# Another order for the row scatters behind the last attention: seven leftovers ahead of the last shift, one batch whole ahead of the next

## The reference

```python
x = x + _L1_attn_ref(_layernorm(x), ...)              # causal attention, 16 heads, 4 groups
x = x + _L1_ffn_ref(_layernorm(x), ...)

def _L1_ffn_ref(hidden, ...):
    logits = flat @ router_w.T                            # 2048 x 32
    scores = jnp.sqrt(jax.nn.softplus(logits))
    _, idx = jax.lax.top_k(scores + expert_bias, K)       # 4 experts for each token
    topv = jnp.take_along_axis(scores, idx, axis=1)
    topv = topv / (topv.sum(axis=-1, keepdims=True) + 1e-20)
    ...
    for each expert: out += p[:, None] * (silu(clip(x @ wg.T)) * clip(x @ wu.T)) @ wd.T
    return out + shared expert
```

## Time and profile before

| | us |
|---|---|
| median of 3 runs | 605.25 |
| lowest and highest run | 604.24, 608.36 |
| span of the profiled execution, first to last instruction | 624.5 |
| TensorE busy in it | 550.5 (88%) |
| VectorE busy | 433.0 (69%) |
| ScalarE busy | 346.5 (55%) |
| GpSimd busy | 241.2 (39%) |

### The profile page before, as it was taken

How to read it: one execution, slowest core, us unless ns; L and a number is a source line. 1 busy time by engine, 2 the same in 40 slices (tenths; PEclk the granted TensorE clock), 3 DMA queues, 4 the chain that set the end, 5 groups by cost and what they waited for, 6 DMA issues and landing times.

```text
span 624.5 us, 14114 instructions
## 1 busy us (share of the span) xinstructions
PE 550.5 (88%) x4231; PEld 390.9 (63%) x4232; DVE 433.0 (69%) x1298; ACT 346.5 (55%) x898; POOL 241.2 (39%) x341
## 2 busy tenths in 40 slices
PE   9998799999879989989998888866589999989996
PEld 4665455665458754666666665534367787778775
DVE  5678858888147886677788683535667777778755
ACT  3533657776826578456675456513146565656672
POOL 2533000000153213266544435556735555555530
PEclk9999979999999999999999899778799999999998
DMA  8599707000680005766505162235545454445498
GB/s 252 179 304 331 211 1 207 3 3 3 192 219 1 2 1 166 209 206 183 229 19 206 62 229 71 70 137 219 170 126 140 140 159 144 151 135 154 143 396 328
DMA packets 49554, 95.24 MB, mean 153 GB/s; under 512 B 8596, under 2 KB 40540, under 8 KB 46940
## 3 DMA queue, kind: packets, MB, share of 16 engines
q1 hardware_dynamic: 41820, 75.34, 39.4%
q0 software_dynamic: 7680, 19.21, 8.2%
HBM read 58.54 MB, written 35.59 MB: 151 GB/s over the span
## 4 chain that ended last, share of the span: by engine, by line
PE 54%; DVE 20%; issue 9%; ACT 6%; DMA 4%; POOL 3%; another core or an unknown queue 2%; SPq 1%; DVEq 0%; ACTq 0%; POOLq 0%
PE banks L1731 7%; PE banks L1513 6%; PE banks L1469 5%; PE banks L1322 4%; PE banks L1742 4%; PE banks L1534 4%; DVE mx L2087 3%; DVE mx L2090 3%; PE banks L1399 3%; PE banks L1794 2%; PE banks L1328 2%; DMA arena<-negT 2%; PE banks L1720 2%; DMA pvs<-rows_by_expert 2%
## 5 line engine op out<-in xcount | busy, mean ns | idle before, releaser
L1162 ACT ACTIVATE arena<-banks 128x512 f32<-128x512 f32 (+1 forms) x256 | 130.1, 550 | 83.3 <-PE banks L1513 45.8
L982 POOL DMA_INDIRECT results_by_rank<-attn_w,goes x80 | 77.3, 966 | 72.2 <-issue 47.9
L1513 PE MATMUL banks<-arena 98*128 98x256 bf16 (+1 forms) x512 | 88.6, 267 | 15.9 <-DVE arena L2186 3.8
L2087 DVE TENSOR_REDUCE mx<-banks 128x4 f32<-128x1024 f32 x64 | 76.0, 1220 | 18.1 <-PE banks L1469 18.0
L922 POOL DMA_INDIRECT rows_by_expert<-arena,bpb x64 | 63.2, 987 | 57.6 <-ACT arena L1162 22.4
L1469 PE MATMUL banks<-arena 96*128 96x256 bf16 (+1 forms) x512 | 81.5, 263 | 4.2 <-DVE mx L2087 2.5
L1731 PE MATMUL banks<-arena,attn_w 128*128 x320 | 84.4, 387 | 0.3 <-issue 0.3
L1513 PEld LDWEIGHTS banks<-arena 98*128 98x128 bf16 x512 | 43.2, 100 | 49.7 <-ACT arena L1162 15.0
L2090 DVE TENSOR_REDUCE mx<-banks 128x4 f32<-128x1024 f32 (+1 forms) x48 | 57.7, 1221 | 22.3 <-PE banks L1473 20.2
L1469 PEld LDWEIGHTS banks<-arena 96*128 96x128 bf16 x512 | 49.9, 99 | 20.0 <-issue 6.0
L1731 PEld LDWEIGHTS banks<-arena,attn_w 128*128 128x128 f32 x320 | 55.6, 194 | 5.1 <-issue 0.7
(11 more groups left out here) (253 smaller groups left out, 1095.7 us busy)
## 6 DMA issues: line engine op xcount, KB each, us to landing
arena<-parts_dram SPq DMA_DIRECT2D x72, 256.0 KB, 4.1
pvs<-rows_by_expert SPq DMA_DIRECT2D x80, 130.0 KB
parts_dram<-arena SPq DMA_DIRECT2D x24, 384.0 KB, 4.8
arena<-results_by_rank SPq DMA_DIRECT2D x6, 1024.0 KB, 10.3
arena<-in SPq DMA_DIRECT2D x2, 2304.0 KB
rows_by_expert<-zero SPq DMA_DIRECT2D x1, 4160.0 KB, 23.6
arena<-in SPq DMA_DIRECT2D x2, 1920.0 KB
arena<-in SPq DMA_DIRECT2D x3, 768.0 KB
```

Source lines behind the costliest of these rows:

```text
L982: pool.indirect_dma_start(ys, bass.IndirectOffsetOnAxis(ap=goes[:, j % 4:j % 4 + 1], axis=0), yb[j % 4], None).then_inc(y_stored[j % 4], 16)
L1162: act.activation(p_ring[n][:, i % P_RING, :], st_bank[RING_AT[n]["s", b, s] % 3][:, 0:P_WIDTH[n]], ACT.Exp, scale=HD ** -0.5).then_inc(exp ...
L1513: ins = pe.matmul(dst[:, at:at + SEQ - q0], keys, q_rows(n, slice(0, ROWS), s, b, q0, SEQ - q0), start=True, stop=(n == 0 or b < POOL_MASKS))
L2087: ins = dve.tensor_reduce(out, src.rearrange("p (q h k) -> p q h k", q=QT, k=nk), AX.X, ALU.max)
```

## The change

The leftovers are split once instead of twice: seven come ahead of the last shift, four behind it, and the wait for the divisions is gone (`scale_rows` still waits for its own statistics). Batch 4 is scattered whole, picks 3, 2, 1, 0, before batch 5, which follows whole in the same order. The number of scatters, their rows and what they raise stay the same. The whole diff:

```diff
--- before.py
+++ after.py
@@ -171,6 +171,7 @@
 RANKS_AT = {(4, 3): 0, (6, 2): 1, (7, 7): 2}
 UP_AT, CLIP_AT, LOGISTIC_AT, HIDDEN_AT, DOWN_AT, ADD_AT = ((6, 7), (6, 9)), (6, 10), ((7, 1), (7, 2), (7, 3)), (7, 5), ((7, 9), (7, 11)), (7, 12)
 SCATTERS = ((68, 13, 8, 16), (99, 11, 8, 16), (122, 9, 8, 5))
+BEHIND_LAST = 7
 
 
 LOGISTICS = 2
@@ -955,19 +956,13 @@
                     for j, n in scatters_at(b * HEADS + h):
                         scatter_nth(j, n, b * HEADS + h)
             tiles = [(BATCHES[2][0] * QT + n // TOPK, n % TOPK) for n in range(SCATTERS[2][3], 4 * TOPK)]
-            for t, k in tiles[:2]:
-                scatter(t, k)
-            pool.wait_ge(divided[1], SEQS * QT)
-            for t, k in tiles[2:4]:
+            for t, k in tiles[:BEHIND_LAST]:
                 scatter(t, k)
             scale_rows(7)
-            for t, k in tiles[4:]:
+            for t, k in tiles[BEHIND_LAST:]:
                 scatter(t, k)
-            scatter_picks(3, (3, 2))
-            scatter_picks(4, (3, 2))
-            for k in (1, 0):
-                scatter_picks(3, (k,))
-                scatter_picks(4, (k,))
+            scatter_picks(3, (3, 2, 1, 0))
+            scatter_picks(4, (3, 2, 1, 0))
             pool.wait_ge(placed[0], 2 * TILES * 16)
             pool.wait_ge(picks_placed, 2)
             pool.nop().then_inc(picks_placed, 1)
```

## The result

The changed kernel takes 613.28 us (median of four runs, 609.34 to 615.94) against 604.75 us (603.81 to 608.36) of the kernel before beside it: a ratio of 1.0126, interval 1.0087 to 1.0166. That is slower by over 1%, and above the upper end of the predicted range, 608.2. Run again at the end of the study, beside 23 runs of the kernel before, it gave 1.0117 [1.0067, 1.0167].

What follows compares the result with a forecast made beforehand. TensorE waits for GpSimd's scatters between attention and the loop: 3.1 us gained at block 4, less a delay of 3.5 - 0.7 - 0.8 = 2.0, gives 1.1 off 605.25, written 604.0 us; range 600.3 to 608.2.

Steps and rivals of the forecast that it cites:

- The gap decides: Between attention and the block loop, 411 to 455 us, TensorE is busy 30.44 of 44 us and waits for GpSimd.
- The second hole: GpSimd idle 3.15 us before 437.98, waiting for the fifth batch's slots; the fourth batch's scatters were to fill it.
- the two unnamed waits: Waits without a named releaser: ScalarE's 5.77 us before its last exponential, VectorE's 3.61 us for the last ranks.
- The term of 5.0 us for an earlier last level: GpSimd's level saying all picks are placed was to come at 449.7 instead of 454.7 us, 5.0 us earlier.
- The levels raised by ScalarE stay where they are within 0.3 us.: ScalarE's two lower levels, at 443.4 and 444.3 us, were to move by no more than 0.3 us.
- Block 4 waits for the last level: In the loop, block 4 starts 9.89 us after block 0, held by GpSimd's last level at 454.7 us.
- the 3.1 us that were to reach the loop: Block 4 could start at 454.1 instead of 457.24 us, so only 3.1 of the 5.0 us help TensorE.
- hold 3.5 us: Five scatters beside the last values and transposes make TensorE's results 3.5 us late, bounds 0 and 4.5.
- second way: If TensorE isn't held, the last shift waits for the five scatters until 417.6 instead of 415.0: delay 2.6 us.
- The rival on the losing side: 17%: TensorE held 4.5 us in its last values and transposes, perhaps 3.6 more at the last ranks; 606.7 to 610.3 us.
- The whole gain arrives: 17%: TensorE isn't held in its last attention step, the stall at the last ranks vanishes; gain 5.7, 599.5 us.
- It doesn't do what it says: 8%: SyncE's slow register operations, not the last level, release block 4; moved scatters only shift the slow stretch: 605.25 us.

Runs made afterwards that it cites:

- e1: The kernel before, unchanged, profiled a second time: ratio 0.9989, span 604.8 us.
- e3: Kernel before with only the fourth batch whole ahead of the fifth, leftover scatters and wait for the divisions kept: ratio 1.0065, 610.86 us.
- e2: Kernel before with seven leftover scatters ahead of the last shift, no wait for the divisions, old order of batches: ratio 1.0072, 610.46 us.
- e5: Kernel before with three leftover scatters ahead of the last shift, no wait for the divisions, old order of batches: ratio 1.0036, 606.25 us.
- e8: Kernel before without the wait for the divisions, all picks 3 and 2 first, three ahead of the last shift, others filling gaps: ratio 1.0034, 605.89 us.
- e10: Kernel before with the wait for the divisions kept, the shift directly behind it, nine leftover scatters following: ratio 1.0035, 606.46 us.
- e4: Changed kernel with three instead of seven leftover scatters ahead of the last shift, new order of batches: ratio 1.0057, 609.55 us.

## Why the prediction was wrong

**The gap decides, and TensorE waits there for what GpSimd does.** Right: the loss lies in that stretch; the loop behind its first matmul lasts as long as before within 1 us (614.2 - 442.29 = 171.9 after, 604.8 - 433.75 = 171.05 in e1).

**The second hole and the two unnamed waits were taken for the kernel's.** This is the step that failed first. The prediction noted that the profiled execution was 19.2 us longer than the median and went on to make the sum in it. In e1 neither the 3.15-us hole nor the unnamed waits of 5.77 and 3.61 us exist; GpSimd is the busy one all through, so a scatter that goes ahead of another delays it by 1.3 us, and there was no idle time to fill. The term of 5.0 us for an earlier last level had nothing to come from. It shrinks to this: counted from the fifth batch's slots, the last level comes 441.7 - 422.5 = 19.2 us behind them in e1 and 445.7 - 429.9 = 15.8 after, 3.4 us sooner, but it isn't what the loop waits for.

**"The levels raised by ScalarE stay where they are within 0.3 us."** Wrong, and the costliest step of the second half. The fourth batch's high picks were put ahead of the fifth's low ones, and the prediction counted on the hole to take them. With no hole, the second level went from 430.3 - 422.5 = 7.8 us behind the slots to 11.3 (after) and 13.8 (e3), past its 2.4 us of slack. Even in the profile of before that slack was to be read: ScalarE's levels at 443.4 and 444.3 stood 447.35 - 444.3 = 3.05 us ahead of block 0, and the prediction never asked what comes when they are later.

**Block 4 waits for the last level.** Wrong: in e1 block 4 starts at 439.54, 2.2 us ahead of the level, and block 6's transfer, the only one that TensorE waits for there (0.40 us), starts at 440.12 in the chain, ahead of 441.7 too. The first load that follows the level is block 7's, and for it TensorE doesn't wait. That 455.14 follows 454.7 in the first profile was read as a release from the times alone. The floor of 4 x 1.68 = 6.7 us for four blocks was too low as well, since they take 7.88 us in e1 with no wait for the level; the granted clock there is 0.50 from 430.8 to 437.4. After, the level is sooner by 3.4 us of the slots' count, and still block 4 follows block 0 by 448.60 - 440.02 = 8.58 us, against 439.54 - 431.66 = 7.88 in e1 (9.89 in the earlier trace rows). So the 3.1 us that were to reach the loop were not to be had, and with them went the predicted gain of 1.1 us.

**What the five scatters cost.** The term "hold 3.5 us" (bounds 0 to 4.5) fell: 6.26 us from the last exponential to the statistics after, against 6.74 in e1. The "second way" to the same term had the right mechanism, the shift waiting behind the five scatters until the last of them, but sized it at 417.6 - 415.0 = 2.6 us. Measured, the shift goes from 0.7 to 4.5 us behind its statistics, 3.8 us, and the slots 4.95 us (e2: 4.9). The kernel before's 0.7 it had right (415.0 - 414.3). Two things made the sum too small. With the last exponential at 411.0 - 4.5 = 406.5 us, the seventh scatter was put 417.6 - 406.5 = 11.1 us behind it, near the 414.60 - 403.70 = 10.9 us measured; but the statistics were put 414.3 - 406.5 = 7.8 us behind it, a distance from the long execution, and measured it is 410.12 - 403.70 = 6.4, so the shift waits longer. And TensorE's lower clock behind that wait, 1.2 us, has no term.

**The rivals.** The rival on the losing side gave 606.7 to 610.3 us by a hold of TensorE that doesn't exist; the change lost more, by two mechanisms, of which it had neither. Its sign, block 0 over 3 us later, came all the same (440.02 - 410.12 = 29.9 us behind the statistics, against 431.66 - 407.73 = 23.9 in e1), so that sign could not tell a held TensorE from a late shift. The sign of the clock came too, if e1 is the measure: 0.81 in the gap after, 0.92 in e1 (0.78 in the first profile of before). "The whole gain arrives" fell with the hole. "It doesn't do what it says" was right that the last level doesn't release block 4, and wrong that the moved scatters then cost nothing; SyncE's slow register operations (0.68 us), on which it rests, belonged to the first profile too: in e1 those of L761 take 0.05 us at most, from 429.1 us on, while scatters run until 438.3.

**VectorE beside the scatters.** Costed at nothing, rightly as far as these rows show. Two row adds of after on VectorE's timeline, and on GpSimd's the scatters that run beside them:

```profile
391.81 0.69 DVE L2192 TENSOR_TENSOR arena<-arena 128x512 f32<-128x512 f32 x1
...
408.02 0.69 DVE L2192 TENSOR_TENSOR arena<-arena 128x512 f32<-128x512 f32 x1
```

```profile
391.75 0.96 POOL L923 DMA_INDIRECT rows_by_expert<-arena,bpb  x1 [0.30 <-ACT arena L1157]
...
408.18 1.36 POOL L923 DMA_INDIRECT rows_by_expert<-arena,bpb  x1 [0.30 <-issue]
```

At 408.02 the row add starts first and takes 0.69 us, as in e1, and it is the scatter beginning under it that lasts 1.36 instead of 0.96 us. That is the half of the lock in the Trainium skill ("SBUF — State Buffer", section "SBUF: two separate sides"; for a VectorE instruction with two SBUF inputs it holds only against a GpSimd instruction that reads SBUF) that the prediction had seen. At 391.75 the scatter starts first, and the row add, 0.06 us behind it, takes its 0.69 us and ends before the scatter does; so the other half, a row add that waits for a scatter, doesn't show here.

**What stays open.** e5, e8 and e10 start the shift 0.65 us sooner and have a + b near 26 us, but run 2.1 to 2.2 us longer than before by the ratio, with intervals that begin just above 1. For e10 its profile has 0.7 of them in a + b (b is 1.05 longer, a 0.3 shorter) and 0.9 in TensorE's wait for block 7. For e5 and e8 it wasn't found where they go; e8's profile is as long as e1's (604.9 against 604.8 us) and has the same a + b, with 0.2 us of TensorE's waiting for block 7. e4's profile shows 5.1 us against 3.4 timed. The start of the gap also moves between executions (the last statistics at 404.9 to 410.3 us in these profiles), and what sets that wasn't looked for. None of these versions beats the kernel before.

## What to carry to other kernels

Hold the profiled execution against the timed runs before a wait in it is read: this one, 3% longer than the median, had waits that the other profiles of the kernel and its versions don't have, and the idle time in it was no room to move work into. On a queue that is never idle, a move ahead is a delay for all that it passes; so for each instruction that is passed write down who waits for it and with how much slack, the small ones first (here a power of 0.7 us that the last sequence's norm and routing need, and four scatters that two levels need). When a change has two moves, run each alone and then more of each: here that gave each loss a term of its own.

## What the runs showed of the hardware

Of 23 row scatters in a row in e1 most start 1.26 to 1.27 us after the one before, and the mean is 1.305, though only 0.96 us of it is busy: the time of the queue, not the busy time, is what each one costs all that stands behind it. From the start of the scatter to ScalarE's level it was 2.55 us in e1 (427.75 to 430.3) and 3.5 after (437.61 to 441.1). A scatter that began under a row add of VectorE lasted 1.36 instead of 0.96 us; a row add that began under a scatter took its usual 0.69. After an idle time of 4.69 us in the changed kernel TensorE ran at a granted clock of 0.50 from 416.8 to 423.5 us, and the same matmuls took 1.09 and 1.89 us that take 0.60 and 1.05 at 1.00. An execution of the kernel before can be 20 us longer than the others with waits of 3.6 to 5.8 us in it whose releaser the trace doesn't name; what caused them wasn't found.
